# A graph network's node loop: products as two 64-row tiles, bias by a small bf16 product, and a sort of packed pairs

## The reference

```python
edge_index = jnp.stack([src, dst])
x = _layernorm(x + _L0_gnn_ref(x, gate_w, gate_b, src, dst))          # gated sum over edges
x = _layernorm(x + _L1_gnn_ref(x, edge_index, W1, as1, ad1, b1,       # two attention layers
                               W2, as2, ad2, b2))
x = _layernorm(x + _L2_gnn_ref(x, beta, src, dst))                    # cosine attention, rows = src
x = _layernorm(x + _L3_gnn_ref(x, edge_index, edge_attr, Wl, bl, Wn, bn))

def gat_layer(x, src, dst, W, a_s, a_d, b, concat):
    h = (x @ W).reshape(N, H, C)
    logits = leaky_relu(alpha_s[src] + alpha_d[dst], 0.2)
    a = softmax of logits over the edges of each dst
    out = segment_sum(h[src] * a[:, :, None], dst)
    return (out if concat else out.mean(axis=1)) + b
```

## Time and profile before

| | us |
|---|---|
| median of 3 runs | 3852.58 |
| lowest, highest run | 3822.3, 3858.96 |
| profiled execution, whole | 3840.28 |
| its span, first to last instruction | 3838.4 |
| busy: PE, PEld | 1557.6, 1281.3 |
| busy: DVE, ACT, POOL | 2397.1, 1237.8, 2309.1 |

### The profile page before, as it was taken

The page is one execution under the profiler, slowest core; times in us unless marked ns, Lnnn a source line. Parts: engine busy times, 40 slices in busy tenths (PEclk is TensorE's granted clock), DMA queues, the critical chain, the costliest instruction groups (busy, mean ns, idle before and its releaser), DMA issues. The chain is left out here.

```text
span 3838.4 us, 34161 instructions
## 1 busy us (share of the span) xinstructions
PE 1557.6 (41%) x5666; PEld 1281.3 (33%) x5666; DVE 2397.1 (62%) x5448; ACT 1237.8 (32%) x3433; POOL 2309.1 (60%) x2220
## 2 busy tenths in 40 slices
PE   1888888887322135650254200000000005785221
PEld 1888888886222124430121100000000004663221
DVE  5555556656987678767898533333885444558553
ACT  0555555552233135440255322222001004553110
POOL 5777777777740377306760177777206776770777
PEclk9999999999999996555677655555555557776555
DMA  2555555665210134322464255555100006783000
GB/s 50 166 165 166 167 167 178 191 185 155 73 39 29 34 76 129 113 83 62 113 182 135 80 154 153 151 153 153 30 0 17 20 20 184 232 232 95 19 18 17
DMA packets 246930, 420.84 MB, mean 110 GB/s; under 512 B 75727, under 2 KB 83169, under 8 KB 245592
## 3 DMA queue, kind: packets, MB, share of 16 engines
q1 hardware_dynamic: 175930, 354.91, 30.1%
q0 software_dynamic: 70912, 65.07, 8.1%
HBM read 185.19 MB, written 236.81 MB: 110 GB/s over the span
## 5 line engine op out<-in xcount | busy, mean ns | idle before, releaser
L579 PE MATMUL banks<-node_w,x_t 65*125 65x200 f32 x1600 | 553.6, 537 | 0.0
L579 PEld LDWEIGHTS banks<-node_w,x_t 65*125 65x125 f32 x1600 | 516.6, 330 | 4.3
L226 POOL DMA_INDIRECT edge_rows<-x_rows,norm_s x400 | 426.2, 1066 | 141.2 <-issue 121.3
L792 PE MATMUL banks<-ident,cross_in 125*65 125x125 f32 (+4 forms) x26 | 11.2, 430 | 1133.9 <-DVE cross_in L815 744.8
L792 PEld LDWEIGHTS banks<-ident,cross_in 125*65 125x65 f32 (+4 forms) x26 | 3.9, 149 | 1139.4 <-DVE cross_in L815 747.1
L242 POOL DMA_INDIRECT out_dram<-n_out,scat_i x200 | 222.1, 1111 | 148.3 <-DVE n_out L2143 86.3
L242 POOL DMA_INDIRECT x_rows<-r_x,src_scat_i x200 | 223.0, 1115 | 125.4 <-DVE r_x L2037 63.4
L622 DVE TENSOR_REDUCE n_var<-n_sq 125x8 f32<-125x512 f32 x125 | 85.6, 686 | 300.3 <-ACT n_sq L636 300.3
L226 POOL DMA_INDIRECT tops<-norm_rows,src_i x200 | 202.6, 1013 | 72.8 <-issue 70.1
L226 POOL DMA_INDIRECT edge_rows<-x_rows,key_i x200 | 199.5, 998 | 77.4 <-issue 60.7
L242 POOL DMA_INDIRECT norm_rows<-edge_rows,scat_i x200 | 205.3, 1027 | 66.7 <-issue 63.3
(11 more groups left out here) (458 smaller groups left out, 5014.3 us busy)
## 6 DMA issues: line engine op xcount, KB each, us to landing
h_rows<-r_h SPq DMA_DIRECT2D x125, 462.0 KB
x_rows<-r_x SPq DMA_DIRECT2D x125, 241.5 KB
x_rows<-r_x SPq DMA_DIRECT2D x125, 224.0 KB
r_x<-x_rows SPq DMA_DIRECT2D x125, 224.0 KB
x_rows<-n_out SPq DMA_DIRECT2D x125, 224.0 KB
n_in<-in_x_dram SPq DMA_DIRECT2D x100, 224.0 KB
x_mixed_edge_rows<-e_dup SPq DMA_DIRECT2D x50, 448.0 KB
r_x<-x_rows SPq DMA_DIRECT2D x50, 241.5 KB
```

Source lines behind the costliest of these rows:

```text
L226: g.indirect_dma_start(out=to[:, j, :], out_offset=None, in_=table, in_offset=bass.IndirectOffsetOnAxis(ap=idx[:, j:j + 1], axis=0)).then_ ...
L579: done = pe.matmul(product[h][:, n // 2, n % 2, :], x_t[u][:, at:at + P], node_w[:, :], start=True, stop=True)
L792: pe.transpose(crossings["bank"][0:cols, 0:rows], frm, ident[0:rows, 0:rows]).then_inc(s_tout, 1)
```

## The change

**Node products.** `transposed_rows` now transposes two nodes at once (128 rows out, four transposes per chunk). Node column 2c lies in rows 0 to 63 and column 2c+1 in rows 64 to 127 of `x_t`, and `node_w` stands twice, in rows 0 to 63 and 64 to 127. A product uses one half of the rows: even nodes the upper tile with bank 2h, odd nodes the lower tile with bank 2h+1. The bias is no longer a 65th row. It is added by a bf16 product of `ones_pair` with `node_bias`, whose first three rows in each half are the three bf16 parts, repeated twice, and whose others are zero; it opens the accumulation in each bank. The preamble gets the transfers that fill these tiles.

**Packed sort.** Key and payload are packed into one 32-bit word (key above bit 15, payload below, with an offset and a gap that keep the pattern a finite number) and compared as f32, so an exchange is one `min` and one `max`. Padding sorts to the front, and the sorted list is read from the end of the buffer. Packing is four instructions at the start, unpacking four at the end.

```diff
-        node_w = sb("node_w", [D + 1, NW])
+        node_w = sb("node_w", [128, NW])
+        node_bias = sb("node_bias", [128, 2 * NW], BF16)
+        ones_pair = sb("ones_pair", [128, P], BF16)
...
-                sp.dma_start(node_w[D:D + 1, :], bias_row[:, :]).then_inc(s_wd, 16)
+                sp.dma_start(node_w[D:2 * D, :], node_w[0:D, :]).then_inc(s_wd, 16)
+                for h in range(2):
+                    for k in range(3):
+                        sp.dma_start(node_bias[h * D + k:h * D + k + 1, :].rearrange("o (c f) -> o c f", f=NW),
+                                     bias_parts[2][:, k].unsqueeze(1).to_broadcast([1, 2, NW])).then_inc(s_wd, 16)
...
-            for c in range(NC):
-                done = pe.transpose(bank[4 + 2 * u + c // 4][0:D + 1, c % 4 * P:c % 4 * P + P], rows[:, c, :], ident[0:P, 0:P])
+            for c in range(NC // 2):
+                done = pe.transpose(bank[4 + u][:, c * P:(c + 1) * P], flat(rows[:, 2 * c:2 * c + 2, :]), ident[0:P, 0:P])
...
-            return nc.scalar.copy(x_t[u][:, :].rearrange("f (b n) -> f b n", b=2), banks[0:D + 1, 4 + 2 * u:6 + 2 * u, 0:NC // 2 * P])
+            return nc.scalar.copy(x_t[u], bank[4 + u][:, 0:NC // 2 * P])
...
-                            for n in range(NC // 2):
-                                at = (h * NC // 2 + n) * P
-                                done = pe.matmul(product[h][:, n // 2, n % 2, :], x_t[u][:, at:at + P], node_w[:, :], start=True, stop=True)
+                            for odd in range(2):
+                                pe.matmul(bank[2 * h + odd][0:P, 0:2 * NW], ones_pair[odd * D:odd * D + D, :], node_bias[odd * D:odd * D + D, :], start=True, stop=False)
+                            for n in range(2):
+                                at = (2 * h + n) * P
+                                for odd in range(2):
+                                    rows = slice(odd * D, odd * D + D)
+                                    done = pe.matmul(product[h][:, odd, n, :], x_t[u][rows, at:at + P], node_w[rows, :], start=False, stop=n == 1)
...
-            dve.tensor_copy(d_srt[0][:, :], di_srt[:, :])
-            v.link(dve.tensor_copy(k_srt[0][:, :], ki_srt[:, :]))
+            v.link(dve.tensor_scalar(high, ki_srt[:, :], float(SKIP_AT), float(SKIP), ALU.is_ge, ALU.mult))
+            v.link(dve.scalar_tensor_tensor(high_i, ki_srt[:, :], float(BASE), high, ALU.add, ALU.add))
+            v.link(dve.tensor_single_scalar(high_i, high_i, LOW_BITS, ALU.logical_shift_left))
+            v.link(dve.tensor_tensor(k_srt[0].bitcast(I32), high_i, di_srt[:, :], ALU.bitwise_or))
...
-                    dve.tensor_tensor(swap, k0[:, :, 0], k0[:, :, 1], ALU.is_gt)
-                    v.link(dve.tensor_tensor(diff, d0[:, :, 1], d0[:, :, 0], ALU.subtract))
-                    v.link(dve.tensor_tensor(diff, diff, swap, ALU.mult))
                     dve.tensor_tensor(k1[:, :, 0], k0[:, :, 0], k0[:, :, 1], ALU.min)
-                    dve.tensor_tensor(k1[:, :, 1], k0[:, :, 0], k0[:, :, 1], ALU.max)
-                    dve.tensor_tensor(d1[:, :, 0], d0[:, :, 0], diff, ALU.add)
-                    done = dve.tensor_tensor(d1[:, :, 1], d0[:, :, 1], diff, ALU.subtract)
+                    done = dve.tensor_tensor(k1[:, :, 1], k0[:, :, 0], k0[:, :, 1], ALU.max)
...
-                        pe.transpose(bank[0][:, part], k_srt[now][:, part], ident[:, :])
-                        ins = pe.transpose(bank[0][:, SF + h * 128:SF + h * 128 + 128], d_srt[now][:, part], ident[:, :])
+                        ins = pe.transpose(bank[0][:, part], k_srt[now][:, part], ident[:, :])
```

More of the change, by code:

```diff
@@ L38 @@
 SORT = 32768
+LOW_BITS, SKIP_AT, SKIP, BASE, PAD_KEY = 15, 64768, 768, 256, 129600
+assert EDGES <= 1 << LOW_BITS and ROWS <= PAD_KEY
 FAR = 1 << 20
@@ L142, in build @@
         ones3 = sb("ones3", [3, 128], BF16)
-        bias_parts = [sb(f"bias_parts{n}", [1, 3, w], BF16) for n, w in enumerate((D, D, W2ROW))]
-        piece = sb("bias_part", [1, W2ROW], BF16)
-        rest = sb("bias_rest", [1, W2ROW])
+        bias_parts = [sb(f"bias_parts{n}", [1, 3, w], BF16) for n, w in enumerate((D, D, NW))]
+        node_bias = sb("node_bias", [128, 2 * NW], BF16)
+        ones_pair = sb("ones_pair", [128, P], BF16)
+        piece = sb("bias_part", [1, NW], BF16)
+        rest = sb("bias_rest", [1, NW])
         wa_pair = sb("wa_pair", [128, 8])
@@ L154, in build @@
         both_x_t = sb("x_t", [128, U * NC * P])
-        x_t = [both_x_t[0:D + 1, u * NC * P:(u + 1) * NC * P] for u in range(U)]
+        x_t = [both_x_t[:, u * NC // 2 * P:(u + 1) * NC // 2 * P] for u in range(U)]
         row_mean = sb("row_mean", [128, 1])
@@ L287, in _ @@
                         sp.dma_start(to[k:k + 1, :].rearrange("o (c f) -> o c f", f=width),
-                                     frm[:, k].unsqueeze(1).to_broadcast([1, times, width])).then_inc(s_wd, 16)
-                sp.wait_ge(s_wd, (4 + 1 + 2 + 9) * 16)
+                                     frm[:, k, 0:width].unsqueeze(1).to_broadcast([1, times, width])).then_inc(s_wd, 16)
+                sp.wait_ge(s_wd, (4 + 1 + 6 + 2 + 9) * 16)
             @block.gpsimd
@@ L309, in _ @@
                 dve.memset(dst_place_i_all, 0)
-                for t in (w1_t_diag, wl_diag, wa_pair, wn_pair):
+                dve.memset(ones_pair[:, :], 1.0)
+                for t in (node_bias, w1_t_diag, wl_diag, wa_pair, wn_pair):
                     dve.memset(t[:, :], 0.0)
@@ L360, in _ @@
                 v.link(dve.memset(ones3[:, :], 1.0))
-                for row, to, w in ((bn_row, bias_parts[0], D), (bl_row, bias_parts[1], D), (bias_row, bias_parts[2], W2ROW)):
+                for row, to, w in ((bn_row, bias_parts[0], D), (bl_row, bias_parts[1], D), (bias_row, bias_parts[2], NW)):
                     v.link(dve.tensor_copy(rest[:, 0:w], row[:, 0:w]))
@@ L907, in build @@
         F_BITS = SF.bit_length() - 1
-        k_srt, d_srt = ([o1_t[:, k * SF:(k + 1) * SF] for k in part] for part in ((0, 1), (2, 3)))
+        k_srt = [o1_t[:, k * SF:(k + 1) * SF] for k in range(2)]
+        high, high_i = o1_t[:, 2 * SF:3 * SF], o1_t[:, 3 * SF:4 * SF].bitcast(I32)
         s_srt, ki_srt, di_srt = (t[:, :, :].rearrange("p k f -> p (k f)") for t in (att_tmp, att1, att2))
@@ L931, in build @@
         PARTS = list(zip(CUTS, CUTS[1:]))
-        held = [t[:, :, :].rearrange("p k f -> p (k f)") for t in (att1, att2)]
+        held = att1[:, :, :].rearrange("p k f -> p (k f)")
         def sort_sp(sp):
@@ L940, in sort_store_sp @@
         def sort_store_sp(sp):
-            sp.wait_ge(s_sorted, len(PARTS))
+            sp.wait_ge(s_sorted, 1)
             for n, frm in enumerate((ki_srt, di_srt)):
@@ L947, in sort_fill_dve @@
             dve.memset(di_srt[:, :], 0)
-            dve.memset(ki_srt[:, :], FAR).then_inc(s_sfill, 1)
+            dve.memset(ki_srt[:, :], PAD_KEY).then_inc(s_sfill, 1)
         def sort_start_dve(dve):
@@ L966, in sort_dve @@
                 hand_over = n + 1 < len(STEPS) and STEPS[n + 1][0] == "turn"
-                k0, k1, d0, d1 = (t[:, :] for t in (k_srt[now], k_srt[1 - now], d_srt[now], d_srt[1 - now]))
+                k0, k1 = k_srt[now], k_srt[1 - now]
                 if what == "direct":
@@ L996, in sort_dve @@
                     v.link(done)
-            dve.tensor_copy(to_k, k_srt[now][:, :])
-            dve.tensor_copy(to_d, d_srt[now][:, :]).then_inc(s_sorted, 1)
+            v.link(dve.tensor_copy(to, k_srt[now]))
         def sort_pe(pe, part):
@@ L1285, in _ @@
                 sort_start_dve(dve)
-                sort_dve(dve, PARTS[0], held[0], held[1])
+                sort_dve(dve, PARTS[0], held)
                 def dots(rows, k, to, chunks):
@@ L1647, in _ @@
                 sort_resume_dve(dve)
-                sort_dve(dve, PARTS[1], held[0], held[1])
+                sort_dve(dve, PARTS[1], held)
                 both = (xa[:, :, 0:D], xa[:, :, 0:D])
@@ L1828, in _ @@
                 sort_resume_dve(dve)
-                sort_dve(dve, PARTS[2], ki_srt, di_srt)
+                sort_dve(dve, PARTS[2], k_srt[0])
+                sort_end_dve(dve)
                 both = (ha[:, :, 0:D], ha[:, :, D:2 * D])
```

27 lines of the change are left out of this document (14 added, 13 removed).

## The result

The changed kernel takes **3668.57 us** (median of four runs, 3662.83 to 3696.62) beside 3851.98 us for the kernel before (3822.3 to 3858.96): a ratio of 0.9557, 95% interval 0.9519 to 0.9594. The forecast was 3670. Measured again in another session it was 3685.70 beside 3849.85, ratio 0.9595 (0.9559 to 0.9632).

What follows compares the result with a forecast made beforehand. GpSimd's gather queue was taken to limit the gain once DVE is faster; 90 us in the first stage, 17 in layer 1 and 67 in layer 2 sum to 174 off 3840.28, giving 3666, adjusted to 3670 us, range 3620 to 3740.

Steps and rivals of the forecast that it cites:

- I put the loop at 13.9 us: Node loop: a turn falls from 15.92 to 13.9 us, saving 100 us, with the loop's end at 787.
- 4.0 us per chunk: Node loop on PE: products 3.3 us with both 64-row tiles streaming together, plus 0.7 us of bias adds.
- The change of mode: Node loop on PE: four changes between 64-row and 128-row use per turn, each a 0.21 us tail, 0.85 us together.
- the flat part: First stage: the loop may be as slow as 14.9 us a turn before the 90 us gain shrinks.
- The clock: Node loop: TensorE works at 1.2 GHz; a rise to 2.4 GHz would leave the time the same, since GpSimd sets it.
- The preamble: Before the loop: six added transfers cost 4.1 us and wider bias splitting about 0.6, in sum 4.7 us.
- The sort: DVE's three sort parts: exchanges fall from 1.78 to 0.53 us, saving 45, 42 and 73 us, none hidden today.
- The gathers' pace: First stage on GpSimd: 120 target columns at 1.45 us each take 174 us, slowed by DVE's scans; target gathers end near 1120.
- Layer 1: First attention layer: DVE is ready 42 us earlier but waits for gathered rows; group two starts 17 us earlier, gain 17 us.
- Layer 2: Second attention layer: 73 us saved less 6 us of waiting for rows at the second group, gain 67 us.
- (1): Rival: the node loop's two tiles don't stream together, path 15.9 or 16.8 us a turn, total 3735 us; chance 0.15.
- (2): Rival: weight loads no longer hidden behind node-loop passes, +8 us a turn, about 4120 us in total; chance 0.03.
- (3): Rival: GpSimd's gathers held up less, 1.35 instead of 1.45 us each, total 3641; chance 0.79 together with the forecast.

Runs made afterwards that it cites:

- e3: Changed kernel with all even-tile products ahead of the odd tile's in each half chunk; 5507.11 us beside 5817.59 for the kernel before, ratio 0.9465.
- e9: Changed kernel with ten unused products added behind the second chunk's products in each node-loop turn; 3678.67 us, ratio interval 0.9541 to 0.9593.
- e1: Kernel before with the packed sort alone, node loop untouched; 5653.36 us beside 5817.59 for the kernel before, ratio 0.9710.
- e10: Changed kernel with 80 of GpSimd's 200 source gathers replaced by one plain transfer of the same size (wrong rows); 3574.47 us, ratio interval 0.9274 to 0.9340.
- e7: The changed kernel again, unaltered, beside the kernel before; 3685.70 us beside 3849.85, ratio interval 0.9559 to 0.9632.
- e8: Changed kernel without the node loop's bias products (output lacks the bias); 3658.92 us beside 3849.85 for the kernel before, ratio interval 0.9480 to 0.9536.
- e2: Kernel before with the node loop's part of the change alone, old sort; ratio 0.9726 to the kernel before, 158 us less.
- e4: Changed kernel with node pairs multiplied in one 128-row product by block-diagonal weights, no 64-row tiles in the loop; 5497.70 us, ratio 0.9451 to the kernel before.
- e11: Kernel before with the node loop's part of the change alone, old sort, run once more; ratio 0.9751 to the kernel before, 151 us less.

## Why the prediction was right, and where it was not

- **The total** was right since its main claim held: what sets the first stage once the loop is faster is GpSimd's queue, so most of the gain beyond 90 us is lost there. Gains by stage, forecast and measured: 90 and 93.1, 17 and 21.8, 67 and 66.4. Of the 174 us, 168 were seen in the profiled execution; the stages behind the layers took 13 us more, which the forecast had at none. That the total came within 2 us is luck: the three stages gained 7 us more than forecast, the rest lost 13, and the second measurement of the same kernel is 17 us higher (3685.70).
- **"I put the loop at 13.9 us"** is the term that was off: 12.15, outside the "13 to 14.5 us" that was to show the prediction right. By its parts: products and adds "4.0 us per chunk" were 3.5 (303.18 to 306.71, a drain of 0.14 in it), because "the PE queue is in order", from which a lone first and last pass followed, is not how two tiles work (e3). ACT's copy-outs, 0.5 us, cost nothing: from the end of the second transposes to the next turn it is 6.7 us, the 7.0 - 0.4 without them. The change of mode was priced somewhat high, 0.21 us for 0.13 to 0.16, and of its four places only two lie in the path. The loop's end was forecast at 787 and came at 693; the forecast did not suffer, because it had said that the gain stops at a loop of 14.9 us. e9, at 13.66, confirms the flat part; nothing was run beyond 14.9.
- **The clock.** The prediction mentioned 2.4 GHz only as a case without effect on the time. It happened, in about half of PE's work in each turn, and it does shorten the turn: in the turns of 11.8 us the clock rises sooner, and the second transposes start 4.01 us behind the first (314.47 to 318.48) instead of 4.55 (302.16 to 306.71). That this leaves the whole time alone follows from the flat part (e9); no run tested it alone.
- **The preamble**: 4.7 forecast, 3.9 measured (first scatter at 83.2 for 79.3). The six transfers took 3.74 us for 4.1.
- **The sort**: 0.53 us per exchange, as forecast. But "None of it is hidden today, as DVE never waits for rows" looked at rows alone. ACT's piece, ready 110 us after the loop's end, takes 20 of the 45 us in the first stage where DVE doesn't wait for rows (e1, e10), so "not 100 + 45 - 4.7 = 140" should have read some 120. It made no difference, since GpSimd's queue ends later still.
- **The gathers' pace**: 120 target columns in 170 us for 174; last gather at 1122.5 for "near 1120". The number was right, but "DVE's scans slow the gathers" is not shown: in e3, in the other condition, the target gathers take 278 us (846.8 to 1124.4) with DVE nearly idle, for 280 in the changed kernel.
- **Layer 1**: group two was forecast for 1400 on before's axis, 17 us earlier; it came 20 earlier, behind a 14.29 us wait for gathered rows. Its ACT wait shrank to 9.2, the later ones kept 13.4. **Layer 2** went as written.
- **Rivals.** (1) and (2) are out by the turn shown above: eight passes in 1.54 us, no exposed load. (3) gathers held up less: hardly, 1.42 us each for 1.45.

## What to carry to other kernels

Before costing a faster loop, read how far the other queues have got when the faster engine arrives: the lead is the most that can be won, and two improvements that each fit into it don't add. A term may then be far off without harm to the total, and such an agreement says nothing of the term. Look at every engine that DVE might then wait for, not only at the one that is latest. Where an engine waits for a small piece of another's work, look at what stands ahead of that piece in its queue; moving it gave 90 us in the two layers beside a kernel before of 5816 us.

## What the runs showed of the hardware

**The output stage differs from run to run, and the clock with it.** From the message stage's first gather to the first output scatter the work is the same in all kernels, but the stretch takes, for before, changed, e7, e8, e9 and e10: 357.7, 366.2, 373.5, 376.7, 387.0 and 348.8 us, at mean granted clocks of 0.72, 0.70, 0.64, 0.68, 0.64 and 0.76. The longest stretches have the lower clocks, though not in strict order (e7 and e8); that the clock is the cause was not tested. Rows of the busy table for two of them, e9 and e10 (columns as in the earlier trace rows; e10's begins 0.3 us late):

```profile
3025.00:3412.00 387.00, 294.73 (x1328) 230.49 (x1328) 220.47 (x414) 182.04 (x406) 205.91 (x200) 0.64 0.66 183
```

```profile
2906.60:3255.10 348.50, 242.61 (x1328) 189.65 (x1328) 218.97 (x415) 180.30 (x406) 210.54 (x200) 0.76 0.72 204
```

The spread of 38 us is as wide as that of the kernel before's runs, and it covers the 8.5 us that the change seemed to lose there.

**A clock row can be wrong.** In before's loop the page shows 9 and the busy table 1.00 while every pass has the duration of 1.2 GHz; e1, with the same loop, shows the same. The runs of the kernel before beside e7 bear this out: two of the seven have a granted mean of 0.73, five of 0.55 to 0.56, and all take 3834 to 3860 us, so the time does not follow the recorded clock. In that loop PE waits 1.6 us a turn and its passes stay at 1.2 GHz. After the change it waits 5 us per turn, works at 1.2 GHz after each wait, and its passes come at 2.4 GHz some 4 to 5 us later.

**The other condition.** In the sessions where the kernel before takes 5810 us the node loop nearly stands while GpSimd issues gathers, and runs at its full 12 us a turn as soon as they end. The sort is slowed too where gathers run beside it, by 4.7 us in many exchanges. Busy table of e2 (PE, PEld, DVE, ACT, POOL), its longest DVE wait in the whole span, and the longest in part two of its sort (total, times, longest, in us; two views, two fences):

```profile
100.00:1000.00 900.00, 74.26 (x384) 52.93 (x380) 75.51 (x155) 61.87 (x184) 676.09 (x662) 0.51 0.13 32
...
1300.00:1400.00 100.00, 56.93 (x394) 45.58 (x390) 77.87 (x167) 63.78 (x196) 0.00 (x0) 0.80 0.71 220
```

```profile
DVE n_var L531 <- issue: 725.3, 16, 66.6
```

```profile
DVE att_tmp L994 <- remote: 71.3, 18, 4.7
```

In the loop DVE, PE and ACT stand for 24 to 67 us at a time with no releaser that the profile knows, while GpSimd's gathers keep their 0.95 us. The waits end at even distances: every 67.2 us in e2's loop (285.97, 353.17, 420.37), two of them a turn, so a turn takes 134 us (not the 70 of e7's expectation); every 89.6 us in e4's (512.31, 601.91, 691.51). e7 and e11 ran on the same chip and met different conditions, so it is not a property of one chip. That the engines wait for their code is a guess; no run here was made to test it, and the two instruction queues of the page moved the same in e11 as in before (71 packets with 0.58 MB, 17 with 0.28 MB).
